# One fused attention and FFN block on one core: the differences of the upper probability blocks one step earlier, one table addition and two products later

## What is computed

```python
xn = _layernorm(x)                                    # x: 1 x 1024 x 256, fp32
qkv = xn @ qkv_w + qkv_b                              # 16 heads of 128
scores = q @ k.T + alibi_mask                         # causal, slope 2 ** (-i / 2) for head i, no 1/sqrt(d)
ctx = softmax(scores) @ v
attn = ctx @ out_w + out_b
gate, up = xn @ lut[gate_idx].T, xn @ lut[up_idx].T   # 688 wide, weights from a table of 16 floats
h = silu(gate) * up
return x + attn + h @ lut[down_idx].T
```

## Time and profile before

| | us |
|---|---|
| runs shown | 542.76, 544.28, 547.27 |
| median | 544.28 |
| the profiled execution | 543.26 |
| its span in the trace | 541.5 |

### The profile page before, as it was taken

How to read it: one execution, slowest core, us unless ns; L and a number is a source line. 1 busy time by engine, 2 the same in 40 slices (tenths; PEclk the granted TensorE clock), 3 DMA queues, 4 the chain that set the end, 5 groups by cost and what they waited for, 6 DMA issues and landing times.

```text
span 541.5 us, 9700 instructions
## 1 busy us (share of the span) xinstructions
PE 493.8 (91%) x2826; PEld 422.4 (78%) x2826; DVE 414.2 (76%) x1067; ACT 360.9 (67%) x657; POOL 403.6 (75%) x312
## 2 busy tenths in 40 slices
PE   7896797999889988998899989997999989789998
PEld 6785576898779876987689768986798779578897
DVE  6796988788888878888788987888788886543541
ACT  3575867687767867595959685877678766824430
POOL 5533989788978998798969897889789979921400
PEclk9997999999999999999999999999999999979999
DMA  8204243332514070606160524134331514000001
GB/s 285 87 0 101 62 98 103 73 91 53 146 44 116 13 186 4 156 0 161 38 144 16 119 80 113 47 79 120 70 90 43 119 38 104 0 1 2 0 21 58
DMA packets 18948, 41.65 MB, mean 77 GB/s; under 512 B 4848, under 2 KB 7024, under 8 KB 18800
## 3 DMA queue, kind: packets, MB, share of 16 engines
q1 hardware_dynamic: 18928, 41.40, 30.2%
HBM read 11.83 MB, written 1.05 MB: 24 GB/s over the span
## 4 chain that ended last, share of the span: by engine, by line
POOL 44%; PE 23%; issue 21%; DVE 7%; ACT 3%; DMA 1%; POOLq 0%; DVEq 0%; ACTq 0%
POOL p_t_lo L1125 17%; POOL w_ffn L1153 15%; POOL work L1118 5%; PE ps_u L447 5%; PE ps_u L449 4%; PE ps_u L448 4%; DVE term L958 3%; PE ps_s L447 2%; PE ps_s L448 2%; PE ps_s L449 2%; POOL v_w_lo L1102 2%; POOL pad L1117 2%; POOL qk_w_lo L1097 2%; ACT ctx_t_hi L721 1%; DVE ctx_t_lo L898 1%
## 5 line engine op out<-in xcount | busy, mean ns | idle before, releaser
L1153 POOL TENSOR_TENSOR w_ffn<-w_ffn,term 128x1088 f32<-128x1088 f32 x60 | 155.0, 2584 | 45.4 <-DVE term L958 45.4
L1125 POOL TENSOR_TENSOR p_t_lo<-p_t_lo,p_t_hi 128x1024 fp32r<-128x1024 f32 (+2 forms) x60 | 133.1, 2251 | 0.0
L738 ACT ACTIVATE work<-work,neg_max 128x128 f32<-128x128 f32 (+7 forms) x128 | 99.0, 773 | 24.1 <-DVE neg_max L937 22.1
L937 DVE CUSTOM_DVE_ANT_0 work<-ps_s,alibi 128x128 f32<-128x128 f32 (+7 forms) x128 | 95.8, 749 | 0.0
L447 PE MATMUL ps_u<-p_t_hi,v_hi 128*128 128x512 f32 x192 | 70.5, 367 | 17.7 <-POOL p_t_lo L1125 17.4
L975 DVE STREAM_TRANSPOSE blocks<-work 128x512 f32<-128x512 f32 x120 | 65.3, 582 | 11.6 <-ACT work L750 11.6
L447 PE MATMUL ps_s<-k_hi,q_hi 128*128 128x256 f32 (+2 forms) x192 | 67.3, 350 | 5.3 <-DVE neg_max L937 5.3
L958 DVE TENSOR_SCALAR term<-codes,entry,table 128x1088 f32<-128x1088 uint8 x60 | 65.8, 1096 | 4.3 <-POOL w_ffn L1153 4.3
L449 PE MATMUL ps_u<-p_t_hi,v_lo 128*128 128x512 f32 x192 | 67.2, 350 | 0.0
L448 PE MATMUL ps_u<-p_t_lo,v_hi 128*128 128x512 f32 x192 | 67.0, 349 | 0.0
L448 PE MATMUL ps_s<-k_lo,q_hi 128*128 128x256 f32 (+2 forms) x192 | 65.8, 343 | 0.0
(11 more groups left out here) (148 smaller groups left out, 1271.1 us busy)
## 6 DMA issues: line engine op xcount, KB each, us to landing
p_t_lo<-blocks SPq DMA_DIRECT2D x240, 116.0 KB, 2.3
qk_raw<-w_qk SPq DMA_DIRECT2D x16, 256.0 KB, 2.7
w_ffn<-idx SPq DMA_DIRECT2D x1, 2176.0 KB, 11.0
v_raw<-w_v SPq DMA_DIRECT2D x8, 256.0 KB, 3.5
o_raw<-w_o SPq DMA_DIRECT2D x8, 256.0 KB, 2.9
out<-acc SPq DMA_DIRECT2D x8, 128.0 KB, 1.7
acc<-x SPq DMA_DIRECT2D x2, 256.0 KB, 3.0
acc<-x SPq DMA_DIRECT2D x1, 512.0 KB, 5.0
```

The source lines that it names most:

```text
L738: act.activation(slot(i), slot(i), ACT.Exp, bias=neg_max[:, col:col + 1], scale=-1.0, accum_out=row_sum[:, col:col + 1]).then_inc(exp_done, 1)
L937: dve.tensor_tensor_reduce(slot(i).rearrange("p (b c) -> p b c", b=banks), made_of, alibi[:, p, S - width:S].rearrange("p (b c) -> p b c", ...
L1125: pool.tensor_tensor(rows, rows.bitcast(F32), chunk_rows(0, chunk).bitcast(F32), ALU.subtract).then_inc(upper_lo, 1)
L1153: pool.tensor_tensor(piece, piece, term[:, :], ALU.add).then_inc(term_added, 1)
```

## The change

Chunks 0 and 1 of the upper blocks are rounded (ACT) and differenced (POOL) in step 3, chunks 2 and 3 in step 4. POOL's second addition moves from step 3 to step 5, DVE's second and third products from steps 3 and 5 to steps 4 and 6. Everything else keeps its place; POOL's `norm` of a step still stands ahead of the differences of that step.

```diff
--- before.py
+++ after.py
@@ -45,8 +45,9 @@
 V_W_AT = 2
 O_W_AT = 7
 ALIBI_AT = 3
-TERM_AT = (1, 3, 5, 7)
-SUM_AT = (1, 3, 6, 7)
+TERM_AT = (1, 4, 6, 7)
+SUM_AT = (1, 5, 6, 7)
+HI_AT = {3: (0, 1), 4: (2, 3)}
 LAG = 3
 
 
@@ -776,8 +777,8 @@
                             exp(n, p, i)
                             if i > QT:
                                 norm(n, p, i - 1)
-                        if i in (4, 5) and not (kind == FIRST and p == 0):
-                            for chunk in (0, 1) if i == 4 else (2, 3):
+                        if i in HI_AT and not (kind == FIRST and p == 0):
+                            for chunk in HI_AT[i]:
                                 upper_hi_of(n, p, chunk)
                         if i == QK_W_AT and kind != LAST:
                             act.wait_ge(qk_landed, n * 32 + (p + 3) * 16)
```

## The result

| | before | after |
|---|---|---|
| median, us | 543.52 | 636.81 |
| the profiled execution, us | 543.26 | 635.92 |
| its span, us | 541.5 | 634.1 |
| mean granted TensorE clock, share of full | 0.987 | 0.922 |

The ratio of the runs is 1.170, with a 95% interval of 1.162 to 1.177: 93 us slower. 636 was forecast, within 606 to 652. Two runs fell into a slow state, one of 943.29 us here and one of 587.96 in e6: they stand in the medians but not in the ratios (the other three of the changed kernel took 635.92 to 637.0).

What follows compares the result with a forecast made beforehand. No single engine was taken as full; a once-per-head loop through the move's landing bounds the kernel. Span 541.5 + 81.8 (rounds) + 10.4 (last head) = 633.7, 635.5 with 1.76 outside it, made 636; range 606 to 652.

Steps and rivals of the forecast that it cites:

- The landing and ACT's wait: ACT, step 3: all landed 11.8 us after first issue; ACT waits 3.7 us in first-kind heads, 0.5 in second.
- The place of the second addition: POOL, steps 3 to 5: behind four differences and the norm it ends at L + 13.25, 10.8 us later than before.
- L: The landing: the time when all DMAs of a move have landed, from which POOL's and DVE's later steps are counted.
- DVE's wait for `term`: DVE, step 6: stands at the third product from about L + 9 and waits some 4 us for the second addition.
- The price of the third product: DVE, step 6: behind POOL's q and k difference it ends 1.9 behind the addition; mask 7 starts 1.8 behind.
- Mask 7 to the next move: Chain from mask 7 through the last transposes to the next move's first issue: 7.3 us.
- The sum of the rounds: Fourteen rounds, each landing delay + 22.35 (one 21.45): 480.2 us where it was 398.4, so 81.8 more.
- The last head: Last head: longer POOL queue, addition ends at L + 15.85, mask 7 starts at L + 19.1, 10.4 us more.
- Only ACT's wait counts: Rival: DVE does not meet the full `term` buffer, only ACT's waiting costs; some 565 to 580 us, chance 0.06.
- Faster: Rival: PE's 17.4 us before the context matmuls go and nothing replaces them; 527 us, chance 0.03.
- no change: Rival: POOL sets the pace and its work is only permuted; 544 us, chance 0.02.
- More than forecast: Rival: products of steps 1 and 4 run into POOL's differences, delaying masks past L + 13.25; 650 us, chance 0.03.

Runs made afterwards that it cites:

- e6: Kernel before with only ACT's roundings moved to steps 3 and 4; POOL's differences and the table as before: 578.6 us (1.061).
- e1: Kernel before with only the table's part: second addition in step 5, products in steps 1, 4, 6, 7; blocks unmoved: 649.1 us (1.191).
- e2: Changed kernel with the second addition back in step 3, ahead of the differences, and the second product back in step 3: 598.5 us (1.099).
- e3: Changed kernel in which addition 1 adds a constant tile instead of the product, so the output is not the reference's: 616.4 us (1.132).
- e4: Changed kernel with POOL's difference of the q and k weights moved from ahead of the second addition to behind it: 626.3 us (1.150).
- e5: Kernel before with only the blocks' part: roundings and differences in steps 3 and 4, table as before: 616.8 us (1.133).
- e8: Kernel before with POOL's v weights' difference (p = 0) in step 5 behind the upper blocks' differences, not in step 2: 552.0 us (1.015).
- e9: e8 with DVE's third product moved ahead of the output sum of step 5 for p = 0: 536.9 us (0.987).

## Why the prediction was right, point by point

**The landing and ACT's wait.** The landing came 11.76 behind the move's start (300.07 less 288.31; 11.8 forecast). ACT waited for it in heads of the first kind, by 1.8 us in the row above and up to 5.3; the forecast 3.7 was too much for the typical head (2.96 is the middle one of the seven), since the head's first steps run a little later now. In the second kind ACT waited in two of the seven rounds (2.13 and 0.78) and not at all in five.

**The place of the second addition.** Forecast to end at L + 13.25, it ended at L + 13.38. The differences took 8.40 together and not 8.8: the 8.8 of the kernel before had the product slipping in between. What stands ahead of and between them took 0.5 more, so the end is 0.13 later than forecast. The lengthening has not gone, it has moved: the second product now slips in ahead of the norm, whose first instruction takes 0.67 us in place of 0.20. The forecast had neither change, and they nearly cancel.

**DVE's wait for `term`.** It is there, 2.39 and 1.80 us, and not the 4 us that were forecast, and it is not the largest wait. In the first kind DVE came later than L + 9 because the second product, in step 4, ran into POOL's first difference and lasted 2.99 (303.62), which the prediction kept for a rival. That did not move mask 7, which hangs on the addition's end. e1 and e2 show that it hangs there; e3 shows that without the buffer POOL's running addition would hold the product nearly as long, which the prediction did not have.

**The price of the third product.** Forecast 1.9 with mask 7 at 1.8 behind the addition; measured 1.80 and 1.76 (315.21 less 313.45). e4 takes exactly this 0.95 away.

**Mask 7 to the next move.** Forecast 7.3; 322.36 less 315.21 is 7.15. PE's waits for the differences went, as said; that PE would wait 52.7 us for DVE's difference of the context unit instead was not said.

**The sum of the rounds.** 480.2 forecast, 483.3 measured, and here errors hide each other. By its own terms the forecast has a mean of 34.15 for the first kind and 34.44 for the second (two of the three long landings fall there). The first kind measures 33.96, so 1.3 us less in seven rounds; the second 35.08, in the rows above up to 36.11, so 4.5 us more. What makes the second kind long is above all one thing: in five of its seven rounds ACT comes to the chunks behind the landing, by 1.71, 0.95, 0.75, 2.05 and 0.98 us, 6.4 in all, and mask 7 is as much later. Shorter landings of the first three moves and the 0.15 a round behind mask 7 hide part of it. And ACT is late in these rounds because PE is. Three windows of the changed kernel, the last two from a move to its landing, with the columns length, busy time of PE, PEld, DVE, ACT and POOL (instructions), granted clock, DMA share and GB/s:

```profile
378.00:391.08 13.08, 7.58 (x43) 6.70 (x42) 9.17 (x20) 7.14 (x12) 7.91 (x5) 0.91 0.00 0
391.08:402.80 11.72, 11.72 (x58) 10.37 (x58) 6.84 (x22) 4.87 (x12) 5.94 (x6) 0.81 0.72 167
322.36:334.10 11.74, 11.74 (x68) 10.63 (x68) 7.96 (x27) 5.44 (x13) 6.63 (x8) 0.93 0.71 164
```

PE at the edge of the first two:

```profile
384.03 0.28 PE L450 MATMUL ps_u<-v_w_hi,xn_t_lo 128*128 128x256 f32 x1
389.82 0.58 PE L448 MATMUL ps_u<-v_w_hi,xn_t_hi 128*128 128x256 f32 x1 [5.50 <-DVE ctx_t_lo L899]
390.20 0.42 PE L449 MATMUL ps_u<-v_w_lo,xn_t_hi 128*128 128x256 f32 x1
```

ACT in the second window and behind it:

```profile
392.79 0.60 ACT L720 ACTIVATE v_hi<-ps_u 128x512 fp32r<-128x512 f32 x1 [3.33 <-PE ps_u L450]
...
404.89 1.99 ACT L757 ACTIVATE p_t_hi<-p_t_lo 128x1024 fp32r<-128x1024 f32 x2
```

PE stands for 5.50 us before a matmul that waits for DVE; it works for 7.58 of the 13.08 us of the first window, at a granted clock of 0.91. In the two windows from a move to its landing it is busy from end to end, at 0.81 and 0.93 of full speed. The same 128x256 matmuls take 0.28 us ahead of the stall and 0.42 behind it. ACT waits for PE's projections (3.33 us in the second window) and comes to the chunks 2.1 behind the landing at 402.83. So the stretch in which PE is the slowest engine runs at a lower clock behind the stall, and its cost comes on top of the stall's own length. The prediction did not have this. That it is the clock, and not the stall alone, fits the other rounds: the five late ones have 0.84, 0.90, 0.93, 0.81 and 0.88 between move and landing, and the shortfall against full clock (1.87, 1.17, 0.78, 2.26 and 1.37 us) rises and falls with ACT's delay. The round of the move at 115.29 has 1.00 there and ACT is not late, and in e5 all of the second kind but the first have 1.00 and in none of them is ACT late. No run sets the clock by itself, so this is argued from rows, not shown by an experiment.

The Trainium skill (TensorE: Matmul & The Clock Gate, What's actually happening) has the clock at one of two levels, 1.2 or 2.4 GHz. By that, a mean of 0.81 is a mixture, with PE at the lower level for 0.38 of the window, an estimate (0.38 x 0.5 + 0.62 = 0.81); the trace agrees in so far as the clock is below 1.00 behind the stall.

**The last head.** ACT's rounding of piece 2 waits for the addition, 6.58 us, and mask 7 starts 18.8 behind the landing; 19.1 was forecast.

```profile
541.78 2.01 ACT L757 ACTIVATE p_t_hi<-p_t_lo 128x1024 fp32r<-128x1024 f32 x2 [1.23 <-DMA p_t_lo<-blocks]
...
557.49 0.63 ACT L804 ACTIVATE qk_w_hi<-w_ffn 128x512 fp32r<-128x512 f32 x1 [6.58 <-POOL w_ffn L1154]
```
```profile
560.61 1.22 DVE L938 CUSTOM_DVE_ANT_0 work<-ps_s,alibi 128x1024 f32<-128x1024 f32 x1
```

**The ends.** The first move starts at 45.67, not at 44.53: 1.1 more, and the prediction had said a few tenths. From the last mask 7 to the end it is 634.1 - 560.6 = 73.5 us, where it was 541.5 - 465.2 = 76.3: 2.8 less, also not forecast. That makes the total agree to 1 us: +3.1 in the rounds, +1.1 ahead of them, -1.0 in the last head (0.7 of it a shorter landing), -2.8 in the tail. The mechanism is shown; the agreement to 1 us is partly luck. Why the tail is shorter stays open: no run was made for it.

**The rivals.** "Only ACT's wait counts" had 565 to 580 us. e6, which does only that, took 578.6, and e2, which has the differences early too, 598.5: the rival had the right size for what it priced, though by other terms than its own (e6 above), but it is not what the change does. "Faster" and "no change" fall by the result. "More than forecast", through products that run into the differences, was half right: the products did run into them, up to 2.99 us each, but DVE still reached the third product ahead of the addition's end, and waited.

## What to carry to other kernels

When an instruction is moved in one engine's queue, look not only for who waits for its result but for who waits for what it frees: here a table addition, whose result no other engine reads before the last head, held the only buffer of a product that stood in front of a softmax. Follow the loop that closes once per head (here move, landing, rounding, differences, addition, product, mask, transposes, move) and price it end to end; that the engines are 56 to 81% busy says nothing about it. Where an operation of DVE starts within a few hundredths of a microsecond of the end of one of POOL's, a run with one of them shifted is worth while: from e8 to e9 that was 15 us of 552.

## What the runs showed of the hardware that was not expected

A DVE tensor_scalar of 128x1088 (uint8 in, fp32 out) that meets a running instruction of POOL ends about 0.6 us behind the end of that instruction: 0.58 behind the difference of the q and k weights (after: 313.48 + 1.80 against 313.40 + 1.30), 0.58 behind an addition (e3), 0.6 behind a difference (e9). Alone it takes 0.84. In the traces of all twelve kernels such a product starts inside a POOL instruction of over 1 us 264 times, and in 250 of them it ends 0.58 to 0.61 behind it. When it slips in between two differences, POOL's four take 8.87 us and not 8.40.

The other 14 were done only 0.6 behind a later instruction of POOL. Twelve of these had come less than 0.1 us ahead of a boundary with POOL's next instruction ready: the seven of e8 (3.01 in the row above), and in the changed kernel the second product at 303.62 (2.99), about 0.04 ahead of the end of POOL's first difference (301.29 + 2.37). But two had come well ahead: the one of 5.82 in e6, 1.65 ahead, and one in the kernel before, which starts at 472.98, 0.54 ahead, and lasts 2.34. So coming early is no guarantee: whichever starts first does not always go first. Why these two were passed over stays open.

PE's granted clock was below 1.00 in the next head behind a stall of one head, 0.81 and 0.93 in the windows above, where ACT came to the chunks 2.05 and 0.75 us behind the landing. Across the runs the mean clock falls, roughly, as the time grows, from 0.990 in e9 (536.9 us) to 0.913 in e1 (649.1 us).
